# Attention of layer 0: one ring of three whole-tile PSUM buffers for scores and turned tiles, whole-tile copies, and a new order on TensorE

## The chip, the cores and the metric

The kernel runs on one core of one Trainium2 chip. The metric is the device time of one execution in microseconds; before the change it is 3761.61 us, the median of 3 runs (3761.56 to 3762.12).

## The reference

The program computes two transformer layers on x of shape (4, 1024, 512). Only the attention of layer 0 is edited. Its mask is all ones, so what it computes for each of the 4 x 16 heads (head size 32) is:

```python
scores = jnp.einsum('bhqd,bhkd->bhqk', q, k) / np.sqrt(hd).astype(np.float32)
scores = scores - torus_dist[:, None, :, :] * torus_scale[None, :, None, None]
attn = jax.nn.softmax(scores, axis=-1)
out = jnp.einsum('bhqk,bhkd->bhqd', attn, v)
```

## The kernel before

Five stages run one after the other, with a barrier of all engines between them: `stage_qkv0`, `stage_attention(K, 0)`, `stage_middle`, `stage_attention1` and `stage_mlp1`. The change is in `stage_attention`, which serves layer 0 alone.

This stage takes the heads as 64 heads of 8 tiles each, 512 tiles `s` in all. A tile is 128 queries by 1024 keys, in float32. Each tile goes through these steps:

- `score(s)`, TensorE, L499: two matmuls of 512 columns write the (negated) scores of the tile into a PSUM buffer of the ring `sp_r`, which has 2 buffers of 128 x 1024 (two banks of PSUM each). Queries and keys are split into a high and a low part, so that 97 rows are contracted.
- `minimum(s)`, VectorE, L599: adds the bias tile `bt` that GpSimd has made (L646), writes the sum to `Sn` in SBUF, one of 5 buffers, and takes the minimum of each row. This frees the score buffer (`s_min`).
- `exponential(s)`, ScalarE, L569: the exponential in place in `Sn`, with the row sums.
- `turn(s)`, TensorE, L531: eight transposes of 128 x 128, four into each of two buffers of the ring `pt_r`, which has 3 buffers of one bank each.
- `copy_turned(s, g, engine)`, ScalarE at L559 or VectorE at L561: copies each half of the turned tile to `PT` in SBUF. The tuple `by_act` says for each half which engine has it: 9 of 16 halves are ScalarE's, and both halves of a head's last tile.
- `times_v(s)`, TensorE, L520: for one block of 128 keys, four products of 32 output columns each (they appear as eight records), accumulated over the 8 blocks of the head in `po`, one bank of PSUM. It runs `V_LAG` = 12 tiles behind the scores.

At the end of a head ScalarE copies `po` to `ov` (L583), TensorE turns it with two transposes (`turn_output`, L507) into another buffer of `pt_r`, and VectorE scales it by the inverse sums into `og` (`output`, L612). The first product of the next head waits for `ov`, since there is one `po`.

Each engine runs its own instructions in the order in which the program writes them, and waits on semaphores at the head of an instruction. A ring's `take` waits until the use of the same buffer one round before is released. So the order in `tensor_program`, `vector_program` and `scalar_program` is the schedule. TensorE goes through the tiles in steps of two: two scores, a turn, (once a head the turn of an output,) two products, a turn. In a step `s`, the turns are those of tiles `s - 4` and `s - 3`.

PSUM is full: 4 banks for `sp_r`, 3 for `pt_r`, 1 for `po`.

Of the kernel before, what the change touches and what calls it, by code (L numbers as in the profile page):

```python
# [7 lines left out]
ACT, ALU, AX = mybir.ActivationFunctionType, mybir.AluOpType, mybir.AxisListType  # L8

P = 128  # L10
B, L, D, H, F = 4, 1024, 512, 16, 2048
HD = D // H
T = B * L
DC, FC, LT = D // P, F // P, L // P
# [390 lines left out]
QW = L // 4  # L405
HALF = LT // 2
N_HEADS = B * H
N_PAIRS = N_HEADS // PAIR
N_TILES = N_HEADS * LT


def stage_attention(K, lay):

    nc, a, pe, dve, act, pool, sp = K.nc, K.a, K.pe, K.dve, K.act, K.pool, K.sp
    bias = lay == 0
    rows_s = 3 * HD + (1 if bias else 0)
    V_LAG = 4 + LT
    by_act = (True, False, True, False) * 3 + (True, False, True, True)
    with Stage(K, f"T{lay}") as S:
        n_ = f"{lay}"  # L420
        qs_l, ks_l = S.loads("QS" + n_, 3, [P, PAIR, L], F32R), S.loads("KS" + n_, 3, [P, PAIR, L], F32R)
# [4 lines left out]
        sums = [S.sb(f"sm{n_}{i}", [P, LT]) for i in range(5)]  # L426
        ov = [S.sb(f"ov{n_}{i}", [P, QW]) for i in range(2)]
        og = S.stores("og" + n_, 2, [P, LT, GRP * HD])
        sp_r = S.ps_ring(f"sp{n_}", 2, [P, L])
        pt_r = S.ps_ring(f"pt{n_}", 3, [P, HALF, P])  # L430
        po = S.ps(f"po{n_}", [P, QW])
        s_score, s_min, s_exp, s_turn, s_pv, s_ov, s_ovT, s_rec, s_out = (S.sem() for _ in range(9))
        s_cp_act, s_cp_dve = S.sem(), S.sem()
        if bias:
# [4 lines left out]

        n_act = [0]  # L440
        for s in range(N_TILES):
            for g in range(2):
                n_act.append(n_act[-1] + by_act[(2 * s + g) % len(by_act)])

        def copied(s, g):
            u = 2 * s + g
            return (s_cp_act, n_act[u + 1]) if by_act[u % len(by_act)] else (s_cp_dve, u + 1 - n_act[u + 1])

        def load_pair(p):
            b, h = p // (H // PAIR), p % (H // PAIR) * PAIR  # L450
# [40 lines left out]
        def score(s):  # L491
            n, t = divmod(s, LT)
            p, j = divmod(n, PAIR)
            qs, ks = qs_l.ready(pe, p), ks_l.ready(pe, p)
            if bias:
                pe.wait_ge(s_one, 1)
            ps = sp_r.take(pe, s, (s_min, s + 1))
            for g in range(L // BLK):
                op = nc.tensor.matmul(ps[:, g * BLK:(g + 1) * BLK], qs[0:rows_s, j, t * P:(t + 1) * P],  # L499
                                      ks[0:rows_s, j, g * BLK:(g + 1) * BLK], start=True, stop=True)  # L500
            op.then_inc(*s_score.up())

        def turn_output(n):
            ps = pt_r.take(pe, ("out", n), (s_out, n + 1))
            pe.wait_ge(s_ov, n + 1)
            for i in range(QW // P):
                op = nc.tensor.transpose(ps[:, i, :], ov[n % 2][:, i * P:(i + 1) * P], K.ident[:])  # L507
            op.then_inc(*s_ovT.up())

        def times_v(s):  # L510
            n, kb = divmod(s, LT)
            p, j = divmod(n, PAIR)
            v = v_l.ready(pe, p)
            for t in range(LT - 2, LT):
                for g in range(2):
                    pe.wait_ge(*copied(n * LT + t, g))
            if kb == 0:
                pe.wait_ge(s_ov, n)
            for g in range(4):
                op = nc.tensor.matmul(po[g * HD:(g + 1) * HD, :], v[:, kb, j * HD:(j + 1) * HD],  # L520
                                      pT[n % 2][:, kb, g * QW:(g + 1) * QW], start=kb == 0, stop=kb == LT - 1)
            if kb == LT - 1:
                op.then_inc(*s_pv.up())

        def turn(s):
            sn = sn_b[s % 5]
            pe.wait_ge(s_exp, s + 1)
            for g in range(2):
                ps = pt_r.take(pe, ("turn", s, g), copied(s, g))
                for i in range(HALF):  # L530
                    op = nc.tensor.transpose(ps[:, i, :], sn[:, (g * HALF + i) * P:(g * HALF + i + 1) * P], K.ident[:])  # L531
                op.then_inc(*s_turn.up())

        def tensor_program():
            for s in range(0, N_TILES + V_LAG + 4, 2):
                if s < N_TILES:
                    score(s)
                    score(s + 1)
                n, t = divmod(s - V_LAG - LT - 2, LT)
                if 0 <= s - 4 < N_TILES:  # L540
                    turn(s - 4)
                if n >= 0 and t == 0:
                    turn_output(n)
                if 0 <= s - V_LAG < N_TILES:
                    times_v(s - V_LAG)
                    times_v(s - V_LAG + 1)
                if 0 <= s - 4 < N_TILES:
                    turn(s - 3)

        def copy_turned(s, g, engine):  # L550
            n, t = divmod(s, LT)
            if by_act[(2 * s + g) % len(by_act)] != (engine is act):
                return
            if n >= 2:
                engine.wait_ge(s_pv, n - 1)
            engine.wait_ge(s_turn, 2 * s + g + 1)
            dst, src = pT[n % 2][:, g * HALF:(g + 1) * HALF, t * P:(t + 1) * P], pt_r.at["turn", s, g][:]
            if engine is act:
                nc.scalar.activation(dst, src, ACT.Copy).then_inc(*s_cp_act.up())  # L559
            else:  # L560
                nc.vector.tensor_copy(dst, src).then_inc(*s_cp_dve.up())  # L561
# [10 lines left out]
        def scalar_program():  # L572
            load_table(nc, 6)
            for s in range(0, N_TILES + V_LAG + 4, 2):
                n, t = divmod(s - V_LAG - LT, LT)
                for i in range(2):
                    if 0 <= s - 2 < N_TILES:
                        exponential(s - 2 + i)
                    if n >= 0 and t == 0 and i == 0:
                        act.wait_ge(s_pv, n + 1)  # L580
                        if n >= 2:
                            act.wait_ge(s_ovT, n - 1)
                        nc.scalar.activation(ov[n % 2][:], po[:], ACT.Copy).then_inc(*s_ov.up())  # L583
                    if 0 <= s - 4 < N_TILES:
                        for g in range(2):
                            copy_turned(s - 4 + i, g, act)

        def minimum(s):
            n, t = divmod(s, LT)
            sn = sn_b[s % 5]  # L590
            if s >= 5:
                dve.wait_ge(s_turn, 2 * (s - 4))
            if t == 0 and n >= 3:
                dve.wait_ge(s_exp, (n - 2) * LT)
            dve.wait_ge(s_score, s + 1)
            m = mn[n % 3][:, t:t + 1]
            if bias:
                dve.wait_ge(s_bias, s + 1)
                nc.vector.tensor_tensor_reduce(sn[:], sp_r.at[s][:], bt[s % 2][:], 1.0, 3.4e38, ALU.add, ALU.min, m).then_inc(*s_min.up())  # L599
            else:  # L600
                nc.vector.tensor_scalar(sn[:], sp_r.at[s][:], 1.0, None, ALU.mult, ALU.min, m).then_inc(*s_min.up())

        def output(n):
            b, h = divmod(n, H)
            buf = og.room(dve, n // GRP)
            two = QW // P
            sm, ps = sums[n % 5], pt_r.at["out", n]
            dve.wait_ge(s_rec, n + 1)
            dve.wait_ge(s_ovT, n + 1)
            hc = slice(h % GRP * HD, (h % GRP + 1) * HD)  # L610
            for i in range(two):
                op = nc.vector.tensor_tensor(buf[:].rearrange("p (g i) d -> p i g d", i=two)[:, i, :, hc],  # L612
                                             ps[:, i, :].rearrange("p (g d) -> p g d", d=HD),
                                             sm[:].rearrange("p (g i) -> p i g", i=two)[:, i, :].unsqueeze(2).to_broadcast([P, LT // two, HD]),
                                             ALU.mult)
            op.then_inc(*s_out.up())

        def vector_program():
            for s in range(0, N_TILES + V_LAG + 4, 2):
                n, t = divmod(s - V_LAG - LT, LT)  # L620
                for i in range(2):
                    if s < N_TILES:
                        minimum(s + i)
                    if n >= 0 and t == 0 and i == 0:
                        dve.wait_ge(s_exp, (n + 1) * LT)
                        nc.vector.reciprocal(sums[n % 5][:], sums[n % 5][:]).then_inc(*s_rec.up())
                    if 0 <= s - 4 < N_TILES:
                        for g in range(2):
                            copy_turned(s - 4 + i, g, dve)
                n, t = divmod(s - V_LAG - LT - 2, LT)  # L630
                if n >= 0 and t == 0:
                    output(n)
# [1677 lines left out]
```

## Time and profile before

| | us |
|---|---|
| median of 3 runs | 3761.61 |
| profiled execution, its own time | 3758.65 |
| its span | 3756.4 |
| TensorE matmul busy in the span | 3552.3 (95%) |
| VectorE busy | 2659.9 (71%) |
| ScalarE busy | 2253.3 (60%) |
| GpSimd busy | 1934.4 (51%) |

The profile is that of one execution. Its engines are PE (TensorE matmuls), PEld (TensorE weight loads), DVE (VectorE), ACT (ScalarE), POOL (GpSimd) and SP (the queue that issues transfers). The busy time of PE counts the records of matmuls, which overlap, so a share of 95% doesn't say that nothing is lost; the distance from one block of matmuls to the next does. The rows are further down.

### The profile page before, as it was taken

To read this page: it belongs to the slowest core of one execution; us is meant where nothing else is said; L and a number is where in the kernel's file an instruction comes from. 1 tells how busy PE (TensorE), PEld (TensorE's weight loads), DVE (VectorE), ACT (ScalarE), POOL (GpSimd) and SP (SyncE) were. 2 spreads that over 40 slices of the span, in tenths; PEclk is the share of its full clock that TensorE was granted. 3 is DMA by queue.
4 is the path that set the end of the run, shared out by engine and by line. 5 is a ranking of instruction groups with operands and counts; after the bars stand their busy time and mean duration, and the time that the engine had idled before them with its cause. 6 is when DMAs were issued, how large, how long until landed. Compare 5 with 4: busy or idle time off the path is not lost. (4 is left out here: it accounts for less than half of the span.)

```text
span 3756.4 us, 67910 instructions
## 1 busy us (share of the span) xinstructions
PE 3552.3 (95%) x25412; PEld 2485.2 (66%) x25412; DVE 2659.9 (71%) x4240; ACT 2253.3 (60%) x3947; POOL 1934.4 (51%) x2189
## 2 busy tenths in 40 slices
PE   8997999999999989899999999799999999994999
PEld 6886776777777758788888875466666666652444
DVE  4335888888888876567675448677777777755997
ACT  2225888888888874433333338555555555554776
POOL 1003555555555533344554547466666666663564
PEclk9998999999999999999999999899999999997999
DMA  5446332233332218757666537924333343314665
GB/s 191 185 163 180 66 71 61 54 69 66 72 66 62 56 44 262 238 185 237 231 231 213 175 130 277 299 55 84 74 66 72 67 85 77 66 33 144 136 140 115
DMA packets 385510, 478.62 MB, mean 127 GB/s; under 512 B 160233, under 2 KB 217069, under 8 KB 385179
## 3 DMA queue, kind: packets, MB, share of 16 engines
q1 hardware_dynamic: 384640, 472.71, 45.3%
q8 instruction: 203, 3.33, 0.4%
q10 hardware_dynamic: 544, 1.58, 0.2%
q14 instruction: 123, 1.00, 0.1%
HBM read 307.67 MB, written 148.93 MB: 122 GB/s over the span
## 5 line engine op out<-in xcount | busy, mean ns | idle before, releaser
L646 POOL TENSOR_SCALAR biastile<-dist,ascale 128x1024 f32<-128x1024 f32 x512 | 577.0, 1127 | 482.1 <-DVE mn L599 474.8
L810 ACT ACTIVATE PT<-st 128x512 f32<-128x512 f32 x1024 | 545.0, 606 | 425.0 <-PE st L744 421.6
L827 DVE TENSOR_REDUCE mn<-s 128x1 f32<-128x1024 f32 x512 | 597.0, 1218 | 271.6 <-PE s L734 271.6
L890 POOL TENSOR_TENSOR two<-PT 128x1024 f32<-128x1024 f32 x256 | 603.4, 2377 | 308.1 <-ACT PT L810 308.1
L599 DVE CUSTOM_DVE_ANT_0 Sn<-sp,biastile 128x1024 f32<-128x1024 f32 x512 | 622.5, 1216 | 73.2 <-PE pt L531 46.6
L569 ACT ACTIVATE Sn<-Sn,mn 128x1024 f32<-128x1024 f32 x512 | 587.1, 1147 | 11.1 <-DVE mn L599 11.1
L531 PEld LDWEIGHTS pt<-ident,Sn 128*128 128x128 f32 x4096 | 455.2, 141 | 177.6 <-issue 151.0
L531 PE MATMUL pt<-ident,Sn 128*128 128x128 f32 x4096 | 547.0, 277 | 22.1 <-DVE og L612 22.1
L559 ACT ACTIVATE PT<-pt 128x512 f32<-128x512 f32 x576 | 337.5, 598 | 136.1 <-PE pt L531 126.2
L744 PE MATMUL st<-QS,KS 98*128 98x512 f32 x1024 | 378.1, 427 | 1.2 <-ACT PT L810 1.2
L734 PE MATMUL s<-KS,QS 96*128 96x512 f32 x1024 | 354.3, 428 | 21.8 <-DMA QS<-s_qlo 20.4
L561 DVE COPY PT<-pt 128x512 f32<-128x512 f32 x448 | 310.0, 692 | 88.0 <-PE pt L531 81.4
L1414 ACT ACTIVATE gf<-pf,b1T 128x512 f32<-128x512 f32 x128 | 88.3, 690 | 414.1 <-PE pf L1295 414.0
L499 PE MATMUL sp<-KS,QS 97*128 97x512 f32 x1024 | 304.6, 418 | 18.3 <-DMA KS<-cpad 13.5
L520 PE MATMUL po<-PT,Vp 128*32 128x256 f32 x4096 | 273.7, 384 | 27.5 <-ACT ov L583 27.5
L744 PEld LDWEIGHTS st<-QS,KS 98*128 98x128 f32 x1024 | 193.0, 189 | 147.6 <-ACT PT L810 65.8
L1376 POOL TENSOR_SCALAR w2h<-w2r 128x512 fp32r<-128x512 f32 x128 | 109.7, 857 | 342.3 <-PE pacc L1307 331.9
L1519 DVE TENSOR_TENSOR gl<-gf,gh 128x512 fp32r<-128x512 f32 x128 | 101.1, 790 | 243.3 <-ACT gh L1418 242.9
L755 PE MATMUL po<-PT,Vp 128*32 128x256 f32 x4096 | 249.0, 384 | 0.0
L734 PEld LDWEIGHTS s<-KS,QS 96*128 96x128 f32 x1024 | 177.8, 194 | 94.8 <-DVE mn L827 50.8
L499 PEld LDWEIGHTS sp<-KS,QS 97*128 97x128 f32 x1024 | 174.2, 191 | 44.9 <-DMA QS<-s_qlo 13.9
L1307 PE MATMUL pacc<-w2h,gl 128*128 128x512 f32 x512 | 199.2, 389 | 0.0
(256 smaller groups left out, 6340.9 us busy)
## 6 DMA issues: line engine op xcount, KB each, us to landing
QS<-s_qhi SPq DMA_DIRECT2D x128, 256.0 KB, 5.0
w1r<-in_L_cond_W_tiles SPq DMA_DIRECT2D x128, 256.0 KB, 4.5
w2r<-in_L_cond_W SPq DMA_DIRECT2D x128, 256.0 KB, 2.8
KS<-s_khi SPq DMA_DIRECT2D x124, 256.0 KB, 6.9
QS<-s_qlo SPq DMA_DIRECT2D x64, 256.0 KB, 6.7
Vp<-s_v SPq DMA_DIRECT2D x64, 256.0 KB, 7.7
s_o<-og SPq DMA_DIRECT2D x32, 512.0 KB, 3.9
KS<-s_klo SPq DMA_DIRECT2D x62, 256.0 KB, 6.0
```

Of the source, the lines that this page charges most:

```text
L499: op = nc.tensor.matmul(ps[:, g * BLK:(g + 1) * BLK], qs[0:rows_s, j, t * P:(t + 1) * P], ks[0:rows_s, j, g * BLK:(g + 1) * BLK], start=Tr ...
L531: op = nc.tensor.transpose(ps[:, i, :], sn[:, (g * HALF + i) * P:(g * HALF + i + 1) * P], K.ident[:])
L559: nc.scalar.activation(dst, src, ACT.Copy).then_inc(*s_cp_act.up())
L561: nc.vector.tensor_copy(dst, src).then_inc(*s_cp_dve.up())
L569: nc.scalar.activation(sn[:], sn[:], ACT.Exp, scale=-1.0, bias=mn[n % 3][:, t:t + 1], accum_out=sums[n % 5][:, t:t + 1]).then_inc(*s_exp.up())
L599: nc.vector.tensor_tensor_reduce(sn[:], sp_r.at[s][:], bt[s % 2][:], 1.0, 3.4e38, ALU.add, ALU.min, m).then_inc(*s_min.up())
L646: nc.gpsimd.tensor_scalar(bt[s % 2][:], dist[:, t, :], K.ascale[:, n % H:n % H + 1], 1.0, ALU.mult, ALU.mult).then_inc(*s_bias.up())
L734: op = nc.tensor.matmul(ps[:, g * BLK:(g + 1) * BLK], qs[0:ROWS, j, t * P:(t + 1) * P], ks[0:ROWS, j, g * BLK:(g + 1) * BLK], start=True, ...
L744: nc.tensor.matmul(ps[:], ks_l.at[p][0][0:ROWS + 2, j, kb * P:(kb + 1) * P], qs_l.at[p][0][0:ROWS + 2, j, g * BLK:(g + 1) * BLK], start=Tr ...
L810: nc.scalar.activation(pT[n % 2][:, kb, g * BLK:(g + 1) * BLK], pst_r.at["st", u, g][:], ACT.Exp, scale=-1.0).then_inc(*s_exp.up())
L827: nc.vector.tensor_reduce(mn[n % 2][:, t:t + 1], ps_r.at[u][:], AX.X, ALU.min).then_inc(*s_min.up())
L890: nc.gpsimd.tensor_tensor(two[m % 6][:], pT[n % 2][:, 2 * k, :], pT[n % 2][:, 2 * k + 1, :], ALU.add).then_inc(*s_two.up())
```

## The change

Scores and turned tiles share one ring, `tile_r`, of three buffers of 128 x 1024 (6 banks). The turned output gets a bank of its own, `p_out`, and `po` keeps its bank. A turned tile is copied whole, by ScalarE or by VectorE: `by_act` now counts tiles, ScalarE has all even tiles, VectorE the odd ones but the sixteenth, which is ScalarE's. The last tile of a head is odd, so that ScalarE has it in every second head. TensorE issues one score, one turn and one product in turn, and the turn of an output between a turn and a product. The waits that counted halves count tiles. At the start of a head's products there is one more wait, on `s_cp_dve`, for all of VectorE's copies of the head.

```diff
-    by_act = (True, False, True, False) * 3 + (True, False, True, True)
+    by_act = (True, False) * 7 + (True, True)
@@
-        sp_r = S.ps_ring(f"sp{n_}", 2, [P, L])
-        pt_r = S.ps_ring(f"pt{n_}", 3, [P, HALF, P])
-        po = S.ps(f"po{n_}", [P, QW])
+        tile_r = S.ps_ring(f"sp{n_}", 3, [P, L])
+        po, p_out = S.ps(f"po{n_}", [P, QW]), S.ps(f"pout{n_}", [P, HALF, P])
@@ def score(s)
-            ps = sp_r.take(pe, s, (s_min, s + 1))
+            ps = tile_r.take(pe, ("score", s), (s_min, s + 1))
@@ def turn_output(n)
-            ps = pt_r.take(pe, ("out", n), (s_out, n + 1))
+            pe.wait_ge(s_out, n)
             pe.wait_ge(s_ov, n + 1)
@@ def times_v(s)
             for t in range(LT - 2, LT):
-                for g in range(2):
-                    pe.wait_ge(*copied(n * LT + t, g))
+                pe.wait_ge(*copied(n * LT + t))
+            pe.wait_ge(s_cp_dve, (n + 1) * LT - n_act[(n + 1) * LT])
@@ def turn(s)
-            for g in range(2):
-                ps = pt_r.take(pe, ("turn", s, g), copied(s, g))
-                for i in range(HALF):
-                    op = nc.tensor.transpose(ps[:, i, :], sn[:, (g * HALF + i) * P:(g * HALF + i + 1) * P], K.ident[:])
-                op.then_inc(*s_turn.up())
+            ps = tile_r.take(pe, ("turn", s), copied(s))
+            for i in range(LT):
+                op = nc.tensor.transpose(ps[:, i * P:(i + 1) * P], sn[:, i * P:(i + 1) * P], K.ident[:])
+            op.then_inc(*s_turn.up())
@@ def tensor_program()
             for s in range(0, N_TILES + V_LAG + 4, 2):
-                if s < N_TILES:
-                    score(s)
-                    score(s + 1)
                 n, t = divmod(s - V_LAG - LT - 2, LT)
-                if 0 <= s - 4 < N_TILES:
-                    turn(s - 4)
-                if n >= 0 and t == 0:
-                    turn_output(n)
-                if 0 <= s - V_LAG < N_TILES:
-                    times_v(s - V_LAG)
-                    times_v(s - V_LAG + 1)
-                if 0 <= s - 4 < N_TILES:
-                    turn(s - 3)
+                for i in range(2):
+                    if s < N_TILES:
+                        score(s + i)
+                    if 0 <= s - 4 < N_TILES:
+                        turn(s - 4 + i)
+                    if n >= 0 and t == 0 and i == 0:
+                        turn_output(n)
+                    if 0 <= s - V_LAG < N_TILES:
+                        times_v(s - V_LAG + i)
@@ def copy_turned(s, engine)
-            engine.wait_ge(s_turn, 2 * s + g + 1)
-            dst, src = pT[n % 2][:, g * HALF:(g + 1) * HALF, t * P:(t + 1) * P], pt_r.at["turn", s, g][:]
+            engine.wait_ge(s_turn, s + 1)
+            dst, src = pT[n % 2][:, :, t * P:(t + 1) * P], tile_r.at["turn", s][:].rearrange("p (k q) -> p k q", q=P)
```

## Rows read from the trace of the kernel before

**Rows 1.** The page: its first line.
```profile
span 3756.4 us, 67910 instructions
```
**Rows 2.** Busy time by stretch: PE, PEld, DVE, ACT, POOL, granted clock, DMA share, GB/s.
```profile
400.00:1300.00 900.00, 858.18 (x7931) 632.43 (x7930) 786.36 (x1414) 785.79 (x1413) 490.24 (x435) 1.00 0.32 65
```
**Rows 3.** Groups by form, 400 to 1300 us: busy us, mean ns, idle time before.
```profile
L599 DVE CUSTOM_DVE_ANT_0 Sn<-sp,biastile 128x1024 f32<-128x1024 f32 x435 | 529.0, 1216 | 40.6 <-PE pt L531 40.6
L569 ACT ACTIVATE Sn<-Sn,mn 128x1024 f32<-128x1024 f32 x435 | 498.8, 1147 | 0.0
...
L531 PE MATMUL pt<-ident,Sn 128*128 128x128 f32 x3477 | 464.6, 276 | 18.8 <-DVE og L612 18.8
...
L559 ACT ACTIVATE PT<-pt 128x512 f32<-128x512 f32 x489 | 286.6, 598 | 114.4 <-PE pt L531 106.0
L561 DVE COPY PT<-pt 128x512 f32<-128x512 f32 x381 | 263.7, 692 | 73.2 <-PE pt L531 67.3
...
L520 PE MATMUL po<-PT,Vp 128*32 128x256 f32 x3472 | 232.3, 385 | 23.0 <-ACT ov L583 23.0
```
**Rows 4.** Timeline, TensorE's matmuls, one head: start us, us, engine, line, operation.
```profile
1105.09 1.04 PE L531 MATMUL pt<-ident,Sn 128*128 128x128 f32 x8
1106.06 1.07 PE L520 MATMUL po<-PT,Vp 128*32 128x256 f32 x16
1107.06 1.09 PE L531 MATMUL pt<-ident,Sn 128*128 128x128 f32 x8
1107.91 1.17 PE L499 MATMUL sp<-KS,QS 97*128 97x512 f32 x4
1108.92 1.04 PE L531 MATMUL pt<-ident,Sn 128*128 128x128 f32 x8
1110.38 1.07 PE L520 MATMUL po<-PT,Vp 128*32 128x256 f32 x16 [0.43 <-ACT ov L583]
...
1113.24 1.04 PE L531 MATMUL pt<-ident,Sn 128*128 128x128 f32 x8
1114.12 0.38 PE L507 MATMUL pt<-ident,ov 128*128 128x128 f32 x2
1114.43 1.07 PE L520 MATMUL po<-PT,Vp 128*32 128x256 f32 x16
...
1116.28 1.17 PE L499 MATMUL sp<-KS,QS 97*128 97x512 f32 x4
1117.80 1.06 PE L531 MATMUL pt<-ident,Sn 128*128 128x128 f32 x8 [0.34 <-DVE og L612]
```
**Rows 5.** Timeline, ScalarE (first three rows) and VectorE of the same head.
```profile
1107.75 1.08 ACT L559 ACTIVATE PT<-pt 128x512 f32<-128x512 f32 x2 [0.30 <-PE pt L531]
1108.72 1.15 ACT L569 ACTIVATE Sn<-Sn,mn 128x1024 f32<-128x1024 f32 x1
...
1109.86 0.38 ACT L583 ACTIVATE ov<-po 128x256 f32<-128x256 f32 x1
...
1104.97 1.22 DVE L599 CUSTOM_DVE_ANT_0 Sn<-sp,biastile 128x1024 f32<-128x1024 f32 x1
...
1106.17 0.69 DVE L561 COPY PT<-pt 128x512 f32<-128x512 f32 x1
1106.77 1.22 DVE L599 CUSTOM_DVE_ANT_0 Sn<-sp,biastile 128x1024 f32<-128x1024 f32 x1
...
1108.75 1.23 DVE L599 CUSTOM_DVE_ANT_0 Sn<-sp,biastile 128x1024 f32<-128x1024 f32 x1 [0.75 <-PE pt L531]
...
1117.17 0.48 DVE L612 TENSOR_TENSOR og<-pt,sm 128x128 f32<-128x128 f32 x2
```
**Rows 6.** Timeline, TensorE's matmuls at the stage's start and its end.
```profile
337.28 0.74 PE L499 MATMUL sp<-KS,QS 97*128 97x512 f32 x2 [0.55 <-DVE mn L599]
...
337.85 1.95 PE L531 MATMUL pt<-ident,Sn 128*128 128x128 f32 x16
...
1391.24 2.80 PE L520 MATMUL po<-PT,Vp 128*32 128x256 f32 x48
```

More of the change, by code:

```diff
@@ L441, in stage_attention, with copied @@
         for s in range(N_TILES):
-            for g in range(2):
[L443 to L447, printed above, removed]
+            n_act.append(n_act[-1] + by_act[s % len(by_act)])
+        def copied(s):
+            return (s_cp_act, n_act[s + 1]) if by_act[s % len(by_act)] else (s_cp_dve, s + 1 - n_act[s + 1])
         def load_pair(p):
@@ L503, in turn_output @@
         def turn_output(n):
-            ps = pt_r.take(pe, ("out", n), (s_out, n + 1))
+            pe.wait_ge(s_out, n)
             pe.wait_ge(s_ov, n + 1)
             for i in range(QW // P):
-                op = nc.tensor.transpose(ps[:, i, :], ov[n % 2][:, i * P:(i + 1) * P], K.ident[:])
+                op = nc.tensor.transpose(p_out[:, i, :], ov[n % 2][:, i * P:(i + 1) * P], K.ident[:])
             op.then_inc(*s_ovT.up())
@@ L527, in turn, with copy_turned @@
             pe.wait_ge(s_exp, s + 1)
-            for g in range(2):
-                ps = pt_r.take(pe, ("turn", s, g), copied(s, g))
-                for i in range(HALF):
-                    op = nc.tensor.transpose(ps[:, i, :], sn[:, (g * HALF + i) * P:(g * HALF + i + 1) * P], K.ident[:])
-                op.then_inc(*s_turn.up())
+            ps = tile_r.take(pe, ("turn", s), copied(s))
+            for i in range(LT):
+                op = nc.tensor.transpose(ps[:, i * P:(i + 1) * P], sn[:, i * P:(i + 1) * P], K.ident[:])
+            op.then_inc(*s_turn.up())
         def tensor_program():
             for s in range(0, N_TILES + V_LAG + 4, 2):
-                if s < N_TILES:
-                    score(s)
-                    score(s + 1)
                 n, t = divmod(s - V_LAG - LT - 2, LT)
-                if 0 <= s - 4 < N_TILES:
-                    turn(s - 4)
-                if n >= 0 and t == 0:
-                    turn_output(n)
-                if 0 <= s - V_LAG < N_TILES:
-                    times_v(s - V_LAG)
-                    times_v(s - V_LAG + 1)
-                if 0 <= s - 4 < N_TILES:
-                    turn(s - 3)
-        def copy_turned(s, g, engine):
+                for i in range(2):
[7 more added lines that the diff above has]
+                        times_v(s - V_LAG + i)
+        def copy_turned(s, engine):
             n, t = divmod(s, LT)
-            if by_act[(2 * s + g) % len(by_act)] != (engine is act):
+            if by_act[s % len(by_act)] != (engine is act):
                 return
@@ L584, in scalar_program @@
                     if 0 <= s - 4 < N_TILES:
-                        for g in range(2):
-                            copy_turned(s - 4 + i, g, act)
+                        copy_turned(s - 4 + i, act)
         def minimum(s):
@@ L591, in minimum @@
             if s >= 5:
-                dve.wait_ge(s_turn, 2 * (s - 4))
+                dve.wait_ge(s_turn, s - 4)
             if t == 0 and n >= 3:
@@ L598, in minimum @@
                 dve.wait_ge(s_bias, s + 1)
-                nc.vector.tensor_tensor_reduce(sn[:], sp_r.at[s][:], bt[s % 2][:], 1.0, 3.4e38, ALU.add, ALU.min, m).then_inc(*s_min.up())
+                nc.vector.tensor_tensor_reduce(sn[:], tile_r.at["score", s][:], bt[s % 2][:], 1.0, 3.4e38, ALU.add, ALU.min, m).then_inc(*s_min.up())
             else:
-                nc.vector.tensor_scalar(sn[:], sp_r.at[s][:], 1.0, None, ALU.mult, ALU.min, m).then_inc(*s_min.up())
+                nc.vector.tensor_scalar(sn[:], tile_r.at["score", s][:], 1.0, None, ALU.mult, ALU.min, m).then_inc(*s_min.up())
         def output(n):
@@ L606, in output @@
             two = QW // P
-            sm, ps = sums[n % 5], pt_r.at["out", n]
+            sm, ps = sums[n % 5], p_out
             dve.wait_ge(s_rec, n + 1)
@@ L627, in vector_program @@
                     if 0 <= s - 4 < N_TILES:
-                        for g in range(2):
-                            copy_turned(s - 4 + i, g, dve)
+                        copy_turned(s - 4 + i, dve)
                 n, t = divmod(s - V_LAG - LT - 2, LT)
```

## The prediction

> **What bounds the kernel now.** I read the page first: a span of 3756.4 us, next to 3758.65 us for the profiled execution and 3761.61 us for the median [rows 1]. The edited stage runs from about 325 to 1395 us. The table by stretches gives its middle, 400 to 1300 us: of 900 us TensorE's matmul records cover 858, VectorE 786, ScalarE 786, all at a granted clock of 1.00, which is the 2.4 GHz level [rows 2]. That says TensorE is nearest to being the bound, but overlapping matmul records hide small gaps, so I went on to the timeline of one head.
>
> 435 tiles in those 900 us are 2.07 us each [rows 3], 16.56 us for the eight tiles of a head; the timeline repeats at this distance (the product that waits for `ov` comes every 16.56 us, one of them at 1110.38). 64 heads make 1060 us, the stage's length. Inside a head I take the distance from the first record of a block to that of the next, which is what the block costs [rows 4]:
> - four score matmuls (two tiles), 1107.91 to 1108.92: 1.01 us
> - turn after scores and before a product, 1105.09 to 1106.06: 0.97 us
> - product of two key blocks, 16 records, 1106.06 to 1107.06: 1.00 us
> - turn after a product and before scores, 1107.06 to 1107.91: 0.85 us
>
> Two tiles cost 3.83 us, a head 4 x 3.83 = 15.32 us. To this come 0.22 us for turning the output (0.88 + 0.31 us where the turn alone takes 0.97), and two waits. The product that opens a head starts 1.46 us after its turn (1108.92 to 1110.38), where 0.97 is usual: 0.49 us for `ov`. The turn after the output's starts 1.52 us after its scores (1116.28 to 1117.80), where 1.01 is usual: 0.51 us for `output`. The sum is 15.32 + 0.22 + 0.49 + 0.51 = 16.54 us, measured 16.56. So nothing else is in a head's time: TensorE's own blocks, 94%, and these two waits, which the groups by form show as idle time behind ACT ov and DVE og [rows 3]. (Their 23.0 and 18.8 us over 54 heads are 0.43 and 0.35 each, a little less than the distances, since records overlap.)
>
> **The change part by part.**
>
> TensorE's order. Every matmul and transpose stays. What changes is how often it passes from one kind to another. Before, two tiles had score (4), turn, product (16), turn. Now each tile has score (2), turn, product (8). Each block from rows:
> - Score block of 2. At the stage's start there is one, followed by a turn: 337.28 to 337.85, 0.57 us [rows 6]. Half of the block of 4 would be 0.505. So two tiles cost 1.14 for 1.01.
> - Turn. The 0.85 us turn ahead of scores no longer exists; every turn now stands between scores and a product, as the 0.97 us one does. So 1.94 for 1.82.
> - Product of 8. A run of 48 records starts at 1391.24 and lasts 2.80 us [rows 6]; less the 0.38 us that one lasts it is 2.42 us for 47 steps, 0.0515 each, while a block of 16 takes 1.00. The rate bounds eight records from 0.41 us; leaving a block costs at most 1.00 - 16 x 0.0515 = 0.18, at least nothing. By the distance of records the halved block lies between 0.50 (nothing for leaving) and 1.00 - 8 x 0.0515 = 0.59. I take 0.58, near the upper end, because the turn starts 1.00 us after the first of sixteen records every time it is not otherwise held up.
>
> A tile is 0.57 + 0.97 + 0.58 = 2.12 us for 1.915 before; bounds 0.505 + 0.91 + 0.50 = 1.915 and 0.57 + 0.97 + 0.59 = 2.13. Eight tiles and the output's turn: 16.96 + 0.22 = 17.18 us. That alone is above the 16.56 us of today with both waits in it.
>
> The wait for `output` goes. It came from the ring `pt_r`: the turned output held one of three halves until VectorE had scaled it. With `p_out` of its own no turn stands behind it: -0.51 us. What is late next is the ring of three tiles. Its sequence is score(s), turn(s-4), score(s+1), turn(s-3), so each take waits for the third use before it. I laid this out, score(s) at 0 with s even, with: minimum ready 0.84 us after its scores start (1107.91 to 1108.75), holding VectorE 1.20 us (1104.97 to 1106.17) and its record 1.23 us; a turned tile ready about 1.13 us after its turn starts (the last of eight transposes starts at 0.85 x 7/8, runs 0.27, and I put 0.1 for being seen) [rows 4, 5].
> - VectorE: minimum(s+1) 2.96 to 4.16, whole copy (s-3) 4.16 to 5.30, next minimum 5.30 where it was ready at 4.24 + 0.84 = 5.08. A pair is 4.24, so minimum(s) starts at 1.06 and frees its tile at about 1.06 + 1.23 + 0.14 = 2.43 (0.14 us is what passes from the end of `ov`'s record, 1109.86 + 0.38, to the product at 1110.38); turn(s-3) asks for it at 2.69. It fits with 0.26 us.
> - score(s+1) needs copy (s-5), free at about 1.3, and asks at 2.12. It fits.
> - ScalarE: copy (s-4) 1.7 to 2.74, two exponentials of 1.14 to 5.02, idle to 5.94.
> Price in a plain pair: nothing, with 0.26 us of cover. Once a head VectorE also does the output (0.48 us, [rows 5]) ahead of a minimum, of which 0.22 us is not covered: I take +0.2 us.
>
> The wait for `ov` changes. ScalarE's copy of `po` stands behind one exponential, 1108.72 to 1109.86, and before that two half copies of the head's last tile [rows 5]. In the new rule `by_act` ScalarE has the last tile only in every second head, but there it is a whole one. Between the last product of a head and the first of the next there used to lie a turn, four score matmuls and a turn (0.85 + 1.01 + 0.97 = 2.83 us); now there lie two score matmuls and a turn, 0.57 + 0.97 = 1.54 us. With score(s) at 0 and the opening product asking at 1.54: in a head whose last tile VectorE copies, ScalarE's exponential runs from -0.36 to 0.78, `ov` to 1.16, product free at 1.30: no wait. Where ScalarE copies it: copy -0.36 to 0.68, exponential to 1.82, `ov` to 2.20, product free at 2.34: 0.80 us. The mean is 0.40 for 0.49 us before. The new wait on `s_cp_dve` adds nothing: that copy is seen at about 1.3. Behind the waiting product stand score(s+1) and everything else of TensorE, so it counts in full.
>
> Whole copies. ScalarE: two half copies in a row hold it 0.97 us (1107.75 to 1108.72); a whole one, from the exponential's 1.147 against 0.598 mean, is some 1.04. VectorE: a half holds it 0.60 us, a whole one 0.60 + 0.53 (the column rate of its 0.692 us record) = 1.14: 0.06 less. The number of tiles per engine stays (4.5 and 3.5 a head). Neither engine sets the pace, so this is worth nothing in the time; what it costs, the later start of the copy, is in the layout above. The Trainium skill, in "VectorE: DVE Perf Modes", section on the TRN2 errata, says that a fixed latency is paid per instruction, so that one large tile pays it once. By that rule the whole copies are a gain, on ScalarE too; the two back-to-back half copies of the trace do not show one there, and the sum stays as it is.
>
> On the switches, the two kinds of turn above differ by 0.12 us for what stands around them [rows 4]. The Trainium skill, "TensorEngine Tiling (Array Packing)", Key Properties, says that changing the tiling mode drains the TensorE, and the product alone uses 32-column tiles. The page has no price; by this rule the change pays for every switch it adds, and the trace's 0.12 us goes with it.
>
> **Sum.** A head: 17.18 + 0.40 + 0.20 = 17.78 us for 16.56, +1.22. Times 64: +78 us, all in this stage. Nothing of the stages after it is touched. On the profiled execution's 3758.65 that is 3837; on the median 3840.
>
> **The rivals.**
> (a) Both waits are absorbed: ScalarE and VectorE run further ahead than in my layout, since TensorE is slower. Then only the blocks count: 17.18 - 16.56 = 0.62 a head, +40 us, 3802. For it: both engines have more slack than before. Against: the order on ScalarE alone forces the wait in every second head.
> (b) The 0.26 us of cover is not there (whole copy or start of a minimum a little later than I put it) and turn(s-3) waits for minimum(s) in every pair. Price 0.2 us more four times a head: +0.8, +51 us on the forecast, 3891. For it: VectorE is the engine in front of two ring uses. Against: its load is about 14.2 of 17 us.
> (c) The other side: switches are free. The 0.12 us of a turn and what follows a product would then be something in the old order (half-tile waits of `pt_r` inside the turns), and leave with it. A tile stays at 1.915: 15.32 + 0.22 + 0.60 = 16.14, -0.42 a head, -27 us, 3735. It decides from (16.56 - 0.22 - 0.60)/8 = 1.968 us a tile: below that the kernel is faster. For it: the two waits do shrink. Against: the score block of 2 at 0.57 us is measured, and the same distances recur in every pair, with no idle time named before them.
> (d) No change: a tile at about 1.968, between (c) and the forecast.
>
> **Chances.** Forecast 0.50 (3815 to 3870), (a) 0.18, (b) 0.16, (d) 0.05, (c) 0.11. Some 0.2% (7.5 us) is about what a measurement of this kernel can tell from no change: faster 0.11, same 0.05, slower 0.84. The range reaches over (a) and (b): 3790 to 3893.
>
> **What would show it.** Timeline of TensorE in a head: score block 0.57, turn 0.97, product 0.58, tile 2.12. No idle time of a turn behind DVE og. The wait behind ACT ov in one head of two, 0.8 us. Little idle time of a turn behind a minimum: if over 0.1 us a pair, (b). A tile under 1.97 us would refute the price of the switches; a granted clock under 1.00 in 400 to 1300 us would be something I did not count.

## The result and the profile after

The changed kernel takes 3818.51 us (median of 4 runs, 3818.28 to 3818.69), the kernel before 3761.59 beside it: a ratio of 1.0151, 95% interval 1.0139 to 1.0163, 57 us slower. The profiled execution took 3818.28 us with a span of 3816.5; before it was 3756.4 [rows 1], so the spans differ by 60 us. The forecast was 3840, range 3790 to 3893, so the change was forecast at +78 us and is +57.

The table by stretches of the changed kernel, 400 to 1300 us (columns as in [rows 2]: PE, PEld, DVE, ACT, POOL, clock, DMA, GB/s):

```profile
400.00:1300.00 900.00, 886.63 (x7504) 579.81 (x7503) 720.69 (x1156) 711.74 (x1107) 464.83 (x412) 1.00 0.29 60
```

GpSimd's count is one bias tile for each tile of scores: 412 for 435 in the same 900 us. VectorE and ScalarE are less busy than before, TensorE more, and the granted clock is 1.00 in both. A clock does not explain the loss; TensorE takes longer for the same matmuls (858.18 us for 435 tiles before, 886.63 for 411). The groups by form of that stretch, to be read beside [rows 3]:

```profile
L591 DVE CUSTOM_DVE_ANT_0 Sn<-sp,biastile 128x1024 f32<-128x1024 f32 x411 | 501.6, 1221 | 179.2 <-issue 179.1
...
L527 PE MATMUL sp<-ident,Sn 128*128 128x128 f32 x3288 | 427.8, 273 | 0.3 <-DVE mn L591 0.3
...
L517 PE MATMUL po<-PT,Vp 128*32 128x256 f32 x3288 | 262.6, 391 | 13.1 <-ACT ov L576 13.1
L552 ACT ACTIVATE PT<-sp 128x1024 f32<-128x1024 f32 x232 | 238.0, 1026 | 188.3 <-PE sp L527 188.3
L554 DVE COPY PT<-sp 128x1024 f32<-128x1024 f32 x180 | 219.6, 1220 | 0.1
```

900 us for 411 tiles are 2.19 us each, 17.52 for a head, where 16.56 was. The idle time of turns behind DVE og (18.8 us before) is gone, that of products behind ACT ov is down from 23.0 to 13.1 us. So the idle time named on TensorE fell by 28 us in this stretch while the kernel became slower: the cost is inside what is counted as busy. The timeline of TensorE shows it, beside [rows 4]:

```profile
1100.17 0.73 PE L496 MATMUL sp<-KS,QS 97*128 97x512 f32 x2
1100.74 1.04 PE L527 MATMUL sp<-ident,Sn 128*128 128x128 f32 x8
1102.28 0.64 PE L517 MATMUL po<-PT,Vp 128*32 128x256 f32 x8 [0.50 <-ACT ov L576]
1102.85 0.73 PE L496 MATMUL sp<-KS,QS 97*128 97x512 f32 x2
1103.41 1.04 PE L527 MATMUL sp<-ident,Sn 128*128 128x128 f32 x8
1104.38 0.64 PE L517 MATMUL po<-PT,Vp 128*32 128x256 f32 x8
1104.95 0.73 PE L496 MATMUL sp<-KS,QS 97*128 97x512 f32 x2
...
1111.48 0.73 PE L496 MATMUL sp<-KS,QS 97*128 97x512 f32 x2
1112.18 1.07 PE L527 MATMUL sp<-ident,Sn 128*128 128x128 f32 x8
```

From start to start a score block is 0.57 us, a turn 0.97, a product 0.57, and a tile 2.10 (1102.28 to 1104.38). Two waits are left. The turn at 1100.74 is followed by its product after 1.54 us instead of 0.97: 0.57 us for `ov`, and this comes in every second head (the next one is without it). Once a head a turn starts 0.70 us after its scores instead of 0.57, at 1112.18. VectorE's timeline shows what it waits for:

```profile
1110.42 0.48 DVE L604 TENSOR_TENSOR og<-pout,sm 128x128 f32<-128x128 f32 x2
1110.82 1.22 DVE L591 CUSTOM_DVE_ANT_0 Sn<-sp,biastile 128x1024 f32<-128x1024 f32 x1
```

The output's scaling holds VectorE 0.40 us and pushes a minimum from 1110.42 to 1110.82; it ends at 1112.04, and 0.14 us later the turn that needs its ring buffer starts. From 1110.42 the minimum would have been over, and the turn free to start, at 1111.78, which is 0.27 us before the turn asks; so 0.13 us of the 0.40 are not covered. The wait for `ov` comes from the order of ScalarE's program, a whole copy, an exponential and then `ov`:

```profile
1099.71 1.03 ACT L552 ACTIVATE PT<-sp 128x1024 f32<-128x1024 f32 x1
1100.63 1.14 ACT L562 ACTIVATE Sn<-Sn,mn 128x1024 f32<-128x1024 f32 x1
...
1101.76 0.37 ACT L576 ACTIVATE ov<-po 128x256 f32<-128x256 f32 x1
```

A head is 8 x 2.105 + 0.22 for the output's turn + 0.57 / 2 + 0.13 = 17.48, measured 17.52.

### The profile page after: what moved, and what is told of

It is laid out like the page before. It is cut to its first block and busy times, and to the rows that moved or that the text cites. A ratio compares the mean times of both kernels' runs of the same rounds, so it can differ in the third digit from the quotient of the medians.

```text
span 3816.5 us, 67464 instructions
## 1 busy us (share of the span) xinstructions
PE 3643.1 (95%) x25412; PEld 2463.2 (65%) x25412; DVE 2631.4 (69%) x4016; ACT 2215.4 (58%) x3659; POOL 1936.4 (51%) x2189
## 5 line engine op out<-in xcount | busy, mean ns | idle before, releaser
L527 PE MATMUL sp<-ident,Sn 128*128 128x128 f32 x4096 | 535.0, 273 | 2.2 <-DVE mn L591 2.2
L527 PEld LDWEIGHTS sp<-ident,Sn 128*128 128x128 f32 x4096 | 475.2, 141 | 88.9 <-issue 28.9
L552 ACT ACTIVATE PT<-sp 128x1024 f32<-128x1024 f32 x288 | 295.4, 1026 | 232.6 <-PE sp L527 232.5
L496 PE MATMUL sp<-KS,QS 97*128 97x512 f32 x1024 | 376.0, 449 | 15.0 <-DMA KS<-cpad 13.5
L517 PE MATMUL po<-PT,Vp 128*32 128x256 f32 x4096 | 325.9, 391 | 16.5 <-ACT ov L576 16.5
L496 PEld LDWEIGHTS sp<-KS,QS 97*128 97x128 f32 x1024 | 154.1, 189 | 223.1 <-issue 205.5
L554 DVE COPY PT<-sp 128x1024 f32<-128x1024 f32 x224 | 273.3, 1220 | 2.1 <-PE sp L527 1.7
L746 PE MATMUL po<-PT,Vp 128*32 128x256 f32 x4096 | 247.3, 382 | 0.0
```

The costliest lines, as they stand in the source:

```text
L527: op = nc.tensor.transpose(ps[:, i * P:(i + 1) * P], sn[:, i * P:(i + 1) * P], K.ident[:])
```

## The experiments

Each run was timed beside the kernel before on one chip; the kernel before gave medians of 3759.7 to 3760.5 us there, and ratios are to it. Where two other runs are set against each other, it is by their medians. The theory was that the order on TensorE costs the time, since it passes between kinds of matmul more often, and that the ring and the whole copies matter only through two waits.

### The order alone, and the ring alone

The first kernel is the one before with the changed kernel's `tensor_program` (with `turn` in its old form of two halves) and nothing else. The cut leaves out the conditions:

```diff
-                if s < N_TILES:
-                    score(s)
-                    score(s + 1)
...
+                for i in range(2):
+                    score(s + i); turn(s - 4 + i); (turn_output(n)); times_v(s - V_LAG + i)
```

> The kernel before with its own rings and half-tile copies, and only the new order on TensorE (score, turn, product for each tile). Theory (the order sets the time): blocks of 0.57, 0.97 and 0.57 us, 2.11 a tile and 17.06 a head with the output's turn; the wait for ov about 0.2 a head, that for output next to nothing: 17.26 us a head for 16.56, +45 us, 3807. Rival (the ring of three and the whole copies cost the time): within 10 us of the kernel before.

Measured: 3832.17 us, ratio 1.0193 (1.0178 to 1.0208), +72, where +45 was expected. The order alone costs more than the whole change. The blocks are 0.57, 0.97 and 0.57 us, as expected; the wait for `ov` is 0.20. What the expectation missed is this, on TensorE's timeline:

```profile
1101.23 0.73 PE L499 MATMUL sp<-KS,QS 97*128 97x512 f32 x2
1102.27 1.06 PE L531 MATMUL pt<-ident,Sn 128*128 128x128 f32 x8 [0.31 <-DVE og L609]
```

1.04 us instead of 0.57, 0.47 us for `output`: with three halves in `pt_r` the old wait stays. 17.06 + 0.20 + 0.47 = 17.73 us a head, measured 17.76 (3243 transposes, 405.4 tiles, in 900 us). So what the ring of three with its own `p_out` brings in the new order is most of this 0.47 us: 0.13 is left of it, while the wait for `ov` rises from 0.20 to a mean of 0.285. That is 0.255 us a head or 16 us, and the total change is +72 for the order and -15 for the rest, in this sequence of the two; the next run shows that the two parts do not simply add.

The other half, the changed kernel with the old order:

> The changed kernel (ring of three whole tiles, whole copies, own bank for the turned output) with the old order on TensorE. Theory: blocks are again 3.83 us for two tiles, but in this order turn(s-2) takes the buffer of turn(s-3), which VectorE has free 2.5 us after that turn started at the earliest, while TensorE asks after 0.85 + 1.01 = 1.86: a wait of at least 0.63 us in every pair, 18.1 us a head or more: 3860 or more. Rival (the order alone is the cause, the ring is neutral in any order): 3745 to 3762.

Measured: 3870.52 us, ratio 1.0295 (1.0279 to 1.0310), +110.

```profile
1105.12 1.17 PE L496 MATMUL sp<-KS,QS 97*128 97x512 f32 x4
1106.85 1.06 PE L527 MATMUL sp<-ident,Sn 128*128 128x128 f32 x8 [0.56 <-DVE PT L557]
```

The blocks are those of before, but the turn after the scores starts 1.73 us after them instead of 1.01: 0.72 us for the copy of the turn before it. In a pair without the output's turn it is 0.65, and 0.45 in the one pair of eight where ScalarE makes that copy; at least 0.63 was expected in every pair. (For part of these waits the profile names ScalarE's exponential, which ends only 0.06 us before the copy, 1115.86 and 1115.92 in one case.) The rival, a ring that is neutral in any order, falls: in the old order the first turn of a step takes the buffer of the turn just before it, while with scores and turns in alternation each turn takes the buffer of a score.

### Which part of the order

Two orders in the kernel before, for the two tiles of a step: S is a score, T a turn, P a product. Before: S S T P P T. Products parted: S S T P T P. Scores parted: S T S P P T.

> The kernel before with the two products of a step parted by a turn and the scores still in pairs (score, score, turn, product, turn, product). Theory (each entry to and exit from the product's 32-column form costs about 0.12 us each): 1.01 + 2 x 0.97 + 2 x 0.57 = 4.09 us for two tiles where 3.83 was, 16.58 a head with the output's turn; the waits for ov and output shrink to 0 to 0.25 together: 3763 to 3779. Rival (switches are free, only the waits count): two tiles at 3.83, 15.8 a head, some 3710.

> The kernel before with the two scores of a step parted by a turn and the products still in pairs (score, turn, score, product, product, turn). As many entries to the product's form as before. Theory (a score block pays some 0.06 us more each time it starts): 0.57 + 0.85 + 0.69 + 1.00 + 0.85 = 3.96 us for two tiles, waits 0.6 to 0.7 a head: 16.7 us a head, 3771, with an uncertainty of 8. If a split of the scores costs nothing: two tiles at 3.83, about 3740.

Measured, products parted: 3777.88 us, ratio 1.0048 (1.0031 to 1.0065), +17. TensorE waits for nothing in it, and still two tiles take 4.16 us for 3.83:

```profile
1103.27 1.19 PE L499 MATMUL sp<-KS,QS 97*128 97x512 f32 x4
1104.30 1.04 PE L531 MATMUL pt<-ident,Sn 128*128 128x128 f32 x8
1105.27 0.64 PE L520 MATMUL po<-PT,Vp 128*32 128x256 f32 x8
1105.84 1.09 PE L531 MATMUL pt<-ident,Sn 128*128 128x128 f32 x8
1106.86 0.64 PE L520 MATMUL po<-PT,Vp 128*32 128x256 f32 x8
1107.43 1.19 PE L499 MATMUL sp<-KS,QS 97*128 97x512 f32 x4
```

1.03 + 0.97 + 0.57 + 1.02 + 0.57 = 4.16. A turn between two products takes 1.02 us. So one more visit to the products costs 0.33 us (0.26 was expected). A head is 4 x 4.16 + 0.22 = 16.86 us; both waits of before are gone, which hides most of the price in the total.

Measured, scores parted: 3788.10 us, ratio 1.0075 (1.0060 to 1.0090), +28. Both expectations were wrong in the total, 3771 with an uncertainty of 8 and, for a split that costs nothing, 3740; the first was wrong for the blocks (3.96) and the second for the waits:

```profile
1108.54 1.09 PE L531 MATMUL pt<-ident,Sn 128*128 128x128 f32 x8
1109.39 0.71 PE L499 MATMUL sp<-KS,QS 97*128 97x512 f32 x2
1109.94 1.04 PE L531 MATMUL pt<-ident,Sn 128*128 128x128 f32 x8
1110.73 0.71 PE L499 MATMUL sp<-KS,QS 97*128 97x512 f32 x2
1111.38 1.07 PE L520 MATMUL po<-PT,Vp 128*32 128x256 f32 x16
1112.38 1.09 PE L531 MATMUL pt<-ident,Sn 128*128 128x128 f32 x8
```

0.85 + 0.55 + 0.79 + 0.65 + 1.00 = 3.84 us for 3.83: parting the scores is free in this order. What the shorter score blocks lose, the turn between them gives back (0.79). The +28 us are waits: the turn after an output waits 0.96 us and the opening product 0.48, together 1.44 us a head for 1.00 before, and 0.44 x 64 = 28.

```profile
1104.57 0.71 PE L499 MATMUL sp<-KS,QS 97*128 97x512 f32 x2
1106.08 1.06 PE L531 MATMUL pt<-ident,Sn 128*128 128x128 f32 x8 [0.81 <-DVE og L613]
...
1114.57 0.72 PE L499 MATMUL sp<-KS,QS 97*128 97x512 f32 x2
1115.70 1.07 PE L520 MATMUL po<-PT,Vp 128*32 128x256 f32 x16 [0.41 <-ACT ov L584]
```

The two totals alone would have blamed the scores (+28) over the products (+17); the blocks say the opposite.

### Is it the 32-column form?

These two runs leave out the real product: its four matmuls of 32 columns are replaced by four of full width against the identity, in the kernel before without its two waits (next section). The call goes on in a second line, which is left out here:

```diff
-                op = nc.tensor.matmul(po[g * HD:(g + 1) * HD, :], v[:, kb, j * HD:(j + 1) * HD],
+                op = nc.tensor.matmul(po[:], K.ident[:],
```

> Leaves out the real product: its four products of 32 columns are replaced by four matmuls of 128 columns against the identity, all into po; the kernel before without its two waits, in its old order (scores in pairs, products in pairs). To be compared with the next run. Eight matmuls for two tiles one after the other, about 3.4 us where 1.0 was: some 6.2 us for two tiles, near 4300.

> Leaves out the real product in the same way, with the two products of a step parted by a turn, as in the run products_split. Theory (it is the 32-column form that is entered and left at a price): parting full-width products costs at most 0.05 us a pair, under 13 us on the run before. Rival (any parting of a block costs): 0.33 us a pair, +84 us.

Measured: 4286.79 and 4288.60 us, with overlapping runs (4285.5 to 4288.4 and 4287.6 to 4289.6). The same parting that costs 0.33 us a pair with products of 32 columns costs at most some 1.8 us in the whole kernel here, 0.007 us a pair. Both orders have a pair in 6.14 us (1103.45 to 1109.59 and 1105.38 to 1111.52); in the parted one:

```profile
1107.37 1.89 PE L520 MATMUL po<-PT,ident 128*128 128x256 f32 x8
1109.10 1.04 PE L531 MATMUL pt<-ident,Sn 128*128 128x128 f32 x8
1109.98 1.89 PE L520 MATMUL po<-PT,ident 128*128 128x256 f32 x8
```

The turn between two of these takes 0.88 us, where it takes 1.02 between products of 32 columns. So a parted block costs nothing by itself; the price comes with the four 32-column groups. The distances say where it lies. Beside full-width products a turn before a product takes 0.88 us and a turn after one 0.79; beside the 32-column products of the kernel before it is 0.97 and 0.85. With the 0.18 us that the prediction gave as the most for leaving a product block (1.00 - 16 x 0.0515), that is an estimate of 0.09 + 0.06 + 0.18 = 0.33 us for a visit.

One thing is not separated: the full-width products also last longer, 1.73 us for eight records where the 32-column ones take 0.57. That short blocks alone would cost as much is argued against by the run with parted scores, in which full-width blocks of 0.55 and 0.79 us alternate and a pair takes 3.84 us for 3.83; a run with short full-width products was not made. The Trainium skill, "TensorEngine Tiling (Array Packing)", Key Properties, says that a change of the tiling mode drains the TensorE. It has no figure; the 0.33 us agree with it, though no trace here shows the drain itself.

### Whole copies and the two waits of the changed kernel

The changed kernel with each copy in two halves, one right after the other on the same engine:

> The changed kernel with each turned tile copied in two halves by the same engine, one after the other; ring, order and semaphores as in the changed kernel. Theory (neither copying engine sets the pace): a copy is longer by about 0.07 us on VectorE and 0.05 on ScalarE, which shows only in the two waits that stand behind a copy, for ov and for the minimum after the output: 0.05 to 0.12 a head, +3 to +8 us on the changed kernel's 3818.5: 3822 to 3827. Rival (whole copies are worth a fixed cost each): more than +15, 3834 or more.

Measured: 3824.27 us, ratio 1.0171 (1.0156 to 1.0186), 6 us over the changed kernel. The two intervals overlap, so this difference rests on the traces. There the wait for `ov` is 0.64 us (1104.29 to 1105.90, 1.61 for 0.97) and the turn behind the output's minimum starts after 0.77 us for 0.57: 0.32 + 0.20 a head for 0.285 + 0.13, 0.105 x 64 = 7. Two halves ahead of the exponential and `ov` hold ScalarE 0.97 us (1103.26 to 1104.23) where the whole copy holds it 0.92; on VectorE, ahead of the output, it is 1.20 (1112.90 to 1114.10) and 1.14 (1109.28 to 1110.42). The whole copies are worth what an earlier end of a copy saves in the two waits, and the traces show nothing beyond it.

The changed kernel with `by_act = (True, False) * 8`:

> The changed kernel with the copies dealt out strictly in turn, so that VectorE has the last tile of every head and ScalarE never has (by_act true, false alone). Theory (the wait for ov in every second head, 0.57 us, comes from ScalarE's copy of the last tile ahead of its exponential): it vanishes, -0.285 a head, -18 us on the changed kernel: 3800. If VectorE gets late by the added copy: 3805 to 3815 with waits of turns behind minima.

Measured: 3802.58 us, ratio 1.0113 (1.0096 to 1.0130), 16 us under the changed kernel. No product waits for `ov`.

Then both waits at once, in either kernel, by moves in the programs of ScalarE and VectorE alone. ScalarE copies `po` before the exponential of its step; VectorE scales the output before the last copy of the step (kernel before) or before its second minimum (changed kernel):

```diff
                 for i in range(2):
+                    if n >= 0 and t == 0 and i == 0:
+                        (wait for s_pv and s_ovT; copy po to ov)
                     if 0 <= s - 2 < N_TILES:
                         exponential(s - 2 + i)
-                    if n >= 0 and t == 0 and i == 0:
-                        (the same)
@@ vector_program
                     minimum(s + i)
                     ...
+                    if m >= 0 and u == 0 and i == 1:
+                        output(m)
                     copy_turned(...)
-                if n >= 0 and t == 0:
-                    output(n)
```

> The changed kernel with the copy of po ahead of the exponential and the output's scaling ahead of the second minimum of its step. Theory: what is left is TensorE's blocks, 8 x 2.105 + 0.22 = 17.06 us a head for 17.50, -28 us on the changed kernel: 3790, still 30 slower than the kernel before. Rival (the waits behind the ring would come back elsewhere): 3800 to 3818.

Measured: 3787.20 us, ratio 1.0069 (1.0054 to 1.0084). 422 tiles in 900 us are 17.06 us a head, the sum of the blocks.

> The kernel before without its two waits and with the changed kernel's order on TensorE: rings and half copies of before. Theory (ring and whole copies matter only through the two waits): 8 x 2.105 + 0.22 = 17.06 us a head, as in the changed kernel without waits: 3787 to 3791, that is +92 to +95 on the same kernel in its old order (3695.7). Rival (the ring or the whole copies are worth something by themselves): over 5 us away from 3787.

Measured: 3790.23 us, ratio 1.0084 (1.0069 to 1.0099), 3 us from the last one, whose interval it overlaps; 3787 to 3791 was expected. With the waits gone, ring, whole copies and `p_out` make no difference to be measured: what is left is the order.

> The kernel before with two moves in the programs of ScalarE and VectorE: the copy of po to ov ahead of the exponential, and the scaling of the output ahead of the last copy of its step. TensorE's order is untouched. Theory (a head is four times 3.83 us of blocks, 0.22 for the output's turn, and the two waits): both waits go, 15.54 us a head for 16.56, -65 us: 3695. Rival (TensorE's blocks already hide other limits; VectorE or ScalarE is next): a part of it, 3715 or more, with new waits behind minima or copies.

Measured: 3695.67 us, ratio 0.9826 (0.9812 to 0.9841), 64 us faster than the kernel before and the fastest of all. The groups by form of TensorE in 400 to 1300 us have no idle time in them:

```profile
L531 PE MATMUL pt<-ident,Sn 128*128 128x128 f32 x3712 | 494.0, 276 | 0.0
...
L520 PE MATMUL po<-PT,Vp 128*32 128x256 f32 x3712 | 248.4, 385 | 0.0
```

3712 turns are 464 tiles, 15.52 us a head, for 15.54 by the sum of the blocks. The same two moves bring 64 us here and 31 in the changed kernel, since here they remove 1.00 us a head and there 0.42 by the distances, 0.46 by the length of a head (17.52 to 17.06). And between these kernels without waits, 3790.2 and 3695.7, the order alone costs 94.5 us, 1.48 us a head, 0.37 a pair: 0.33 for the visit and 0.04 for the rest.

### Fewer visits

> The kernel before without its two waits (as in the run before_no_waits) and with the products in fours: every second step issues four of them between its turns, the other steps none. Theory (each visit to the product's form costs some 0.33 us, whatever its length): half as many visits, -0.66 us a head, -42 us on 3695.7: 3653, if the rings hold. They are short (two score buffers, three halves) and steps are now uneven, 2.9 and 4.7 us: if VectorE cannot follow in the short steps, turns wait for copies and scores for minima, and it ends between 3653 and 3720.

Beyond what the expectation says, the scores are parted by a turn in the steps without products and stay together in the others. Measured: 3760.95 us, ratio 0.9999 (0.9990 to 1.0009): above the 3720 that I had given as the upper end. The blocks are shorter: four products in 1.87 us, four tiles in some 7.4 us for 7.66. But:

```profile
1105.92 0.71 PE L499 MATMUL sp<-KS,QS 97*128 97x512 f32 x2
1107.14 0.73 PE L499 MATMUL sp<-KS,QS 97*128 97x512 f32 x2 [0.51 <-DVE mn L603]
...
1113.28 0.60 PE L531 MATMUL pt<-ident,Sn 128*128 128x128 f32 x4
1114.27 0.66 PE L531 MATMUL pt<-ident,Sn 128*128 128x128 f32 x4 [0.38 <-ACT PT L563]
```

Once a head a score waits for a minimum (54 times in 900 us) and once a turn for a copy (55 times), and a head takes 16.57 us where the blocks alone would make some 15.0. The two rings, two score buffers and three halves, do not cover the uneven steps, and the kernel is 65 us slower than the same with products in pairs. Whether longer rings would bring the gain of fewer visits is not tested, since PSUM is full.

## Why the prediction was right

By its own steps, a head:
- **Blocks.** Forecast 17.18 us, measured 17.06. Score block and turn were 0.57 and 0.97 to the hundredth. The product of eight was put at 0.58 and is 0.57, and the sum of rounded blocks accounts for the rest: 2.105 a tile, not 2.12. This is 8 of the 21 us by which the forecast was high.
- **The wait for `output`** went as described, and the ring of three put a minimum in its place, at the point described. The cover was 0.27 us for 0.26; the output holds VectorE 0.40 us, and I had taken its record of 0.48. So it is 0.13 us for 0.20, 4 us.
- **The wait for `ov`** is in every second head, as laid out, but 0.57 us and not 0.80. Of the 0.23 us, 0.12 are the whole copy, which holds ScalarE 0.92 us (1099.71 to 1100.63), where I had put 1.04 from the exponential's record. Another 0.10 is the start of that copy, 0.46 us before the head's score and not 0.36. Mean 0.285 for 0.40, 7 us.
- **Whole copies** were put at nothing, with the reason that the trace showed no gain on ScalarE. That reason was wrong: the 1.04 was taken from another kind of instruction, and against two halves (0.97) the whole copy gains 0.05 us on ScalarE and 0.06 on VectorE. A gain of this kind is what the Trainium skill states in "VectorE: DVE Perf Modes", section on the TRN2 errata, for one large tile against many small ones; its mechanism is given for sources in SBUF, and its table has a fixed term for sources in PSUM, as here, too. In the time it is worth some 6 us, through the two waits and on both engines together.
- **The sum.** +0.94 a head for +1.22; times 64 it is 60, the difference of the spans.

One reading in the text was wrong though its sum was right. It charged the score blocks 0.13 us a pair for being parted. The run with parted scores has 3.84 us for 3.83, and between parted products (4.16) and the new order (4.21) the parted scores cost 0.05. The rest of the 0.38 us a pair, 0.33, is the price of an additional visit to the 32-column products, whichever block it shows in. The sum came out right because every block was taken with the neighbours that it has in the new order, except that the step from a product to a score was not in any row; it turned out as the step from a product to a turn.

Rival (c), free switches, and (d) are refuted: a tile takes 2.105 us, with no idle time in it, where 1.915 and some 1.968 were their figures, and the two kernels without waits differ by 94.5 us. Rival (a), both waits absorbed, is not what happened (3818 for 3802); the changed kernel comes to that state only when the two instructions are moved, at 3787. Rival (b) did not occur: in a plain pair the turn starts 0.57 us after its scores, and TensorE's idle time behind minima is 0.3 us in 900.

## What to carry to other kernels

Price a reordering by the distances from block to block in the timeline, each with its neighbours, and not by busy time or by idle time with a named releaser: the loss here stood inside time counted as busy (886.63 of 900 us), while named idle time fell. In this kernel 32-column products are cheaper in runs of two key blocks than of one, and four in a run gained nothing, since the rings did not hold; the scores could be parted for 0.05 us a pair or less. Before an order on the bounding engine is changed for the sake of a wait, look at where the awaited instruction stands in its own engine's program; moving two of them gave 64 us, while the change, which by a new order and ring put a wait of 0.13 us in the place of one of 0.51, cost 57.

## What was not expected of the hardware

- Going over from full-width matmuls to four 32-column groups and back cost TensorE 0.33 us a visit at a granted clock of 1.00, and none of it is shown as idle. With full-width products in the same places, which also last longer, the same split cost 0.007 us.
- A whole copy of 128 x 1024 from PSUM holds ScalarE 0.92 us, two halves 0.97; an exponential of the same size from SBUF with its row sums holds it 1.13 in the same trace.
- A turn takes 0.79 us between scores, 0.85 after a product and before scores, 0.97 between scores and a product, and 1.02 between two 32-column products: eight transposes each time.
